# Transposing a masked attention matrix in 32x32 blocks on VectorE and moving the blocks by DMA, in a two-layer graph kernel

## The reference

```python
# layer 0: 4 heads of 64, mask adj[g]
h = relu(layernorm(x))
q, k, v = h @ Wq, h @ Wk, h @ Wv
att = softmax(where(adj, q @ k.T / 8, -FLT_MAX))
x = x + (att @ v) @ Wo + bo
# layer 1: 8 heads of 64, masked where adj is true
h = relu(layernorm(x))
m = h @ map_w.T + map_b
n = m / max(norm(m per head), eps)
cos_adj = (n @ n.T masked) > 0.1
q, k = m @ q_w.T + q_b, m @ k_w.T + k_b
p = softmax(where(mask, -1e10, q @ k.T / 8)) * keep
adj = cos_adj * p
out = relu(((adj @ (h @ gcn_map.T + b)) @ gcn_W.T) / (adj.sum(-1) + 1))
x = x + out
```

## Time and profile before

| | |
|---|---|
| median of 3 runs | 4121.55 us (4118.8 to 4130.23) |
| profiled execution | 4121.26 us, its span 4119.5 us |
| mean granted clock of TensorE | 0.993 |
| PE busy | 95%, 32976 matmuls |
| DVE busy | 63% |
| ACT busy | 48% |
| POOL busy | 32% |
| DMA queue of SP | 110.12 MB, 7.8% of 16 engines |
| x, out, move: each x64, 512 KB | 3.4, 2.8 and 3.1 us from issue to landing |
| adj: x64, 64 KB | 2.6 us from issue to landing |

### The profile page before, as it was taken

How to read it: one execution, slowest core, us unless ns; L and a number is a source line. 1 busy time by engine, 2 the same in 40 slices (tenths; PEclk the granted TensorE clock), 3 DMA queues, 4 the chain that set the end, 5 groups by cost and what they waited for, 6 DMA issues and landing times.

```text
span 4119.5 us, 105002 instructions
## 1 busy us (share of the span) xinstructions
PE 3931.4 (95%) x32976; PEld 3437.0 (83%) x32976; DVE 2608.3 (63%) x9426; ACT 1979.3 (48%) x5583; POOL 1324.3 (32%) x2007
## 2 busy tenths in 40 slices
PE   7999999999999999999999999999999999999997
PEld 6888888888888888888888888888888888888886
DVE  4666666666666666666666666666666666666664
ACT  3554544544545445445454454454454544544544
POOL 3333333333332333333333333333333333333332
PEclk8999999999999999999999999999999999999998
DMA  3000000000000000000000000000000000000000
GB/s 87 16 32 26 22 32 16 32 32 16 32 27 21 32 18 30 32 16 32 29 18 32 22 25 32 16 32 32 16 32 27 21 32 16 32 32 16 32 27 17
DMA packets 65544, 111.77 MB, mean 27 GB/s; under 512 B 20880, under 2 KB 22448, under 8 KB 65520
## 3 DMA queue, kind: packets, MB, share of 16 engines
q1 hardware_dynamic: 64928, 110.12, 7.8%
q0 software_dynamic: 592, 1.35, 0.2%
HBM read 44.34 MB, written 33.55 MB: 19 GB/s over the span
## 4 chain that ended last, share of the span: by engine, by line
PE 65%; DVE 12%; issue 11%; ACT 6%; POOL 4%; DVEq 1%; DMA 1%; POOLq 0%; ACTq 0%; SPq 0%
PE bank L755 34%; PE bank L763 9%; PE bank L748 7%; PE bank L783 6%; PE bank L775 4%; ACT prob L501 3%; PE bank L883 3%; POOL prob L417 2%; DVE x_mid L663 2%; ACT att L475 2%; DVE prob L650 2%; DVE att L607 2%; DVE att L618 1%; POOL rstd L362 1%; DVE hT L640 1%
## 5 line engine op out<-in xcount | busy, mean ns | idle before, releaser
L475 ACT ACTIVATE att<-att,nmax 128x256 f32<-128x256 f32 x1024 | 509.7, 500 | 299.6 <-DVE nmax L607 299.6
L417 POOL TENSOR_SCALAR prob<-prob,rsum 128x256 f32<-128x256 f32 x512 | 241.1, 487 | 631.2 <-DVE rsum L657 628.2
L755 PE MATMUL bank<-hT,w_qkv 128*128 128x256 f32 x3072 | 414.9, 288 | 4.7 <-DVE hT L640 4.7
L755 PE MATMUL bank<-qkm,w_k 128*128 128x256 f32 x3072 | 416.6, 285 | 0.0
L755 PEld LDWEIGHTS bank<-hT,w_qkv 128*128 128x128 f32 x3072 | 376.9, 189 | 37.9 <-issue 24.2
L755 PE MATMUL bank<-hT,w_map 128*128 128x256 f32 x3072 | 396.7, 285 | 5.1 <-DVE hT L640 1.0
L618 DVE SCALAR_TENSOR_TENSOR att<-bank,att 128x256 f32<-128x256 f32 x1024 | 392.3, 420 | 4.0
L755 PE MATMUL bank<-qkm,w_q 128*128 128x256 f32 x3072 | 390.8, 283 | 0.0
L755 PEld LDWEIGHTS bank<-hT,w_map 128*128 128x128 f32 x3072 | 372.5, 189 | 18.4 <-DVE hT L640 17.3
L763 PE MATMUL bank<-w_v,hT 128*128 128x512 f32 x1536 | 385.3, 399 | 0.0
L755 PEld LDWEIGHTS bank<-qkm,w_k 128*128 128x128 f32 x3072 | 380.1, 188 | 5.0
(11 more groups left out here) (122 smaller groups left out, 7949.6 us busy)
## 6 DMA issues: line engine op xcount, KB each, us to landing
x_in<-x SPq DMA_DIRECT2D x64, 512.0 KB, 3.4
x_res<-x_mid SPq DMA_DIRECT2D x64, 512.0 KB, 3.1
out<-x_res SPq DMA_DIRECT2D x64, 512.0 KB, 2.8
adj<-adj SPq DMA_DIRECT2D x64, 64.0 KB, 2.6
att<-gcn_map POOLq DMA_DIRECT2D x2, 512.0 KB, 9.0
x_mid<-wq SPq DMA_DIRECT2D x1, 512.0 KB, 5.6
x_res<-wk SPq DMA_DIRECT2D x1, 512.0 KB, 6.8
v<-wv SPq DMA_DIRECT2D x1, 512.0 KB, 7.7
```

The lines of the kernel that those rows point to most:

```text
L417: last = g.tensor_scalar(prob0[:, hd, c, :], prob0[:, hd, c, :], rsum0[:, hd, c:c + 1], 0.0, ALU.mult, ALU.add)
L475: s_.activation(e_sl, e_sl, ACT.Exp, bias=nmax1[:, p, c, e:e + 1], scale=-1.0, accum_out=esum1[:, p, c, e:e + 1]).then_inc(exp1_done, 1)
L755: last = t_.matmul(dst, w(ws, k)[:, t * 128:t * 128 + 128], rhs[:, rs, k, :], start=(k == 0 and i == 0), stop=(k == KT - 1 and i == 2))
```

## The change

The steps `turn_a` and `turn_b` are gone from TensorE and ScalarE. VectorE has the steps `flip_a` and `flip_b` in their place, one block transpose a head, in place in att: each 32x32 block of the 128x512 values is turned where it lies. Then each block column still has to move to the partition quarter where its row index is now: SP has a step `shift` a pair, 16 DMAs from `att` to `uT`, each from one quarter of 32 partitions to another (or the same), 1 KB a partition, 32 KB in all. A shift begins when both flips of its pair are done and the value product of the pair before has read uT. TensorE's `value` waits until all 16 have landed, and so does `score_a` of the pair after next, which writes the same half of att. So that a DMA finds its 256 numbers in one run, att is laid out with the four blocks quarters outermost, and the operands of score, cos and value are read in runs of 32 columns. `value` and `back` share bank 4, the plain steps have three banks (5 to 7), and all five lists are written anew.

```diff
@@ the lists: one line of TENSOR, and SYNC
-        "ht0a", ("score", 0), "ht0b", ("cos", 0), "qk0", "qk1", ("turn_a", 0), "qk2", ("turn_b", 0), "s0", "s1", ("value", 0),
+        ("score", 0), "ht0a", "ht0b", ("cos", 0), ("score", 1), "qk0", "qk1", "qk2", "qk3", "s0", "s1", ("cos", 1),
...
-    PBANKS = 4
+    PBANKS = 3
     SYNC = [
-        "x", ("out", 0), "move", "adj"
+        ("shift", 0), ("shift", 1), ("shift", 2), "x", ("shift", 3), ("out", 0), "adj", "move"
     ]
...
-        att = sb("att", [128, 2, 2, C, N])
+        att = sb("att", [128, 2, 4, 2, C, C, 32])
...
-        v_bank = gram_bank
+        v_bank = (bank[4], bank[4])
@@ SP
+                    elif kind == "shift":
+
+                        sp.wait_ge(flipped, pairs(a, p, 2) + 2)
+                        sp.sem_inc(passed_sync, 1)
+                        sp.wait_ge(uv_full, pairs(a, p))
+                        sp.sem_inc(passed_sync, 1)
+                        for rows in range(4):
+                            for cols in range(4):
+                                sp.dma_start(uT_blocks[32 * cols:32 * cols + 32, rows, :, :, :, :].rearrange("p e c j f -> p (e c j f)"),
+                                             att[32 * rows:32 * rows + 32, p % 2, cols, :, :, :, :].rearrange("p e c j f -> p (e c j f)")).then_inc(turned[p], 16)
@@ GpSimd
-                        g.tensor_scalar(mask1[:, :, :], adj8[:, :, :], MASKED_L1, 0.0, ALU.mult, ALU.add).then_inc(mask1_ready, 1)
+                        for c in range(C):
+                            g.tensor_scalar(mask1[:, c, :].rearrange("p (b j f) -> p b j f", j=C, f=32),
+                                            adj8[:, c, :].rearrange("p (j b f) -> p b j f", j=C, f=32), MASKED_L1, 0.0,
+                                            ALU.mult, ALU.add).then_inc(mask1_ready, 1)
@@ ScalarE
-                            e_sl = att[:, p % 2, e, c, :]
+                            e_sl = att[:, p % 2, :, e, c, :, :].rearrange("p b j f -> p b (j f)")
...
-                    elif kind in ("turn_a", "turn_b"):
-                        e = "ab".index(kind[5])
-                        act.wait_ge(t_full, pairs(a, p, 2) + e + 1)
-                        act.wait_ge(uv_full, pairs(a, p))
-                        s_.activation(uT[:, e, :], t_bank[e][:, :], ACT.Copy).then_inc(uT_ready, 1)
@@ VectorE
+                        if e == 0:
+                            dve.wait_ge(turned[(p + 2) % 4], BLOCK_MOVES * (a + (1 if p < 2 else 2)))
+                            dve.sem_inc(passed_vector, 1)
...
+                    elif kind in ("flip_a", "flip_b"):
+
+                        e = "ab".index(kind[5])
+                        dve.wait_ge(gated, pairs(a, p, 4) + 2 * e + 2)
+                        dve.sem_inc(passed_vector, 1)
+                        blocks = att[:, p % 2, :, e, :, :, :].rearrange("p b c j f -> p b (c j f)")
+                        v_.transpose(blocks, blocks).then_inc(flipped, 1)
@@ TensorE
+            def by_quarter(ap, source):
+
+                return ap.rearrange("p (j b f) -> p b j f", j=C, f=32) if source else ap.rearrange("p (b j f) -> p b j f", j=C, f=32)
...
-                            last[e] = t_.matmul(banks[e][:, c * N:c * N + N], left[r, ls, c * 128:c * 128 + 128], right[r, rs, :],
-                                                start=(i == 0), stop=(i == 2))
+                            last[e] = t_.matmul(order(banks[e][:, c * N:c * N + N], False), left[r, ls, c * 128:c * 128 + 128],
+                                                order(right[r, rs, :], True), start=(i == 0), stop=(i == 2))
...
-                        pe.wait_ge(uT_ready, pairs(a, p, 2))
-                        head_products(score_bank, q1[:, :, p, :], k1[:, :, p, :])[1].then_inc(score_full, 1)
+                        pe.wait_ge(masked, pairs(a, p, 4))
+                        head_products(score_bank, q1[:, :, p, :], k1[:, :, p, :], by_quarter)[1].then_inc(score_full, 1)
...
+                    elif kind == "value":
+                        pe.wait_ge(turned[p], BLOCK_MOVES * (a + 2))
                         pe.wait_ge(rel_done, pairs(a, p))
...
-                        values(v_bank[0][:, 0:N], v1, 2 * p, lambda e, jc: uT[:, e, jc * N:jc * N + N]).then_inc(uv_full, 1)
+                        values(v_bank[0][:, 0:N], v1, 2 * p, lambda e, jc: uT_blocks[:, :, e, :, jc, :].rearrange("p r c f -> p c r f")).then_inc(uv_full, 1)
```

More of the change, by code:

```diff
@@ L62, in gnn_two_layers @@
-        ("turn_b", 2), ("value", 2), "ht1a", "ht1b", ("exp_a", 3), "m0", ("exp_b", 3), "m1", ("turn_a", 3), "m2",
-        ("turn_b", 3), "m3", "q2", ("value", 3), "q1", "k1", "q0", "k0", "q3", "k3", "k2"
[4 rows of a table added]
     ]
     VECTOR = [
-        "ht0a", "ht0b", ("score_a", 0), ("score_b", 0), ("cos_a", 0), "qk0", ("cos_b", 0), "qk1", "s0", "qk2", "s1",
-        ("factor", 0), "sum0", ("back", 0), "sum1", "qk3", ("score_a", 1), ("score_b", 1), "s2", ("cos_a", 1), "s3",
-        ("cos_b", 1), "sum2", "sum3", "v0", ("factor", 1), ("back", 1), "av", ("score_a", 2), ("score_b", 2), ("cos_a", 2),
[3 rows of a table removed]
+        ("score_a", 0), ("score_b", 0), "ht0a", "ht0b", ("cos_a", 0), ("flip_a", 0), ("cos_b", 0), "qk0", ("flip_b", 0),
@@ L72, in gnn_two_layers @@
+        ("score_a", 1), "qk1", "qk2", ("score_b", 1), ("factor", 0), "qk3", "s0", ("cos_a", 1), "s1", "sum0", "s2", "s3",
+        ("flip_a", 1), "sum1", ("cos_b", 1), "sum2", ("flip_b", 1), "sum3", "v0", ("back", 0), ("factor", 1), ("score_a", 2),
+        ("score_b", 2), ("cos_a", 2), ("cos_b", 2), ("flip_a", 2), ("factor", 2), "av", ("flip_b", 2), ("score_a", 3),
[3 rows of a table added]
     ]
     POOL = [
-        ("unit", 0), "mid", "mask0", "sum0", "sum1", ("unit", 1), ("back", 0), "sum2", "sum3", "rstd1", ("back", 1),
@@ L75, in gnn_two_layers @@
-        ("back", 2), "m0", "rstd0", "m1", "m2", "m3", "pow", "mask1", ("back", 3)
+        "mask0", ("unit", 0), "mid", ("unit", 1), "sum0", "sum1", "sum2", "sum3", ("back", 0), "rstd1", ("back", 1), "m0",
+        "m1", ("back", 2), "mask1", "rstd0", "m2", "m3", "pow", ("back", 3)
     ]
-    PBANKS = 4
+    PBANKS = 3
     SYNC = [
-        "x", ("out", 0), "move", "adj"
+        ("shift", 0), ("shift", 1), ("shift", 2), "x", ("shift", 3), ("out", 0), "adj", "move"
     ]
     PRODUCTS = [s for s in TENSOR if isinstance(s, str)]
-    bank_of = {s: 4 + k % PBANKS for k, s in enumerate(PRODUCTS)}
+    bank_of = {s: 5 + k % PBANKS for k, s in enumerate(PRODUCTS)}
@@ L230, in gnn_two_layers @@
         gated = count("gated")
-        t_full = count("t_full")
-        uT_ready = count("uT_ready")
+        flipped = count("flipped")
+        turned = [count(f"turned{p}") for p in range(PAIRS1)]
         uv_full = count("uv_full")
@@ L286, in _ @@
                 sp.dma_start(adj8[:, :, :], adj[0].rearrange("(c p) j -> p c j", p=128)).then_inc(adj_loaded, 16)
+                for p in range(PAIRS1):
+                    sp.sem_inc(turned[p], BLOCK_MOVES)
                 for k, (src, _) in enumerate(PIECES):
@@ L856, in body @@
                         for t in range(PAIRS0):
-                            last = values(full[:, t * N:t * N + N], v0, 2 * t, lambda e, jc: ptm[:, 2 * t + e, jc * N:jc * N + N])
+                            last = values(full[:, t * N:t * N + N], v0, 2 * t, lambda e, jc: ptm[:, 2 * t + e, jc * N:jc * N + N].rearrange("p (c r f) -> p c r f", c=C, f=32))
                         last.then_inc(product_full, 1)
```

42 lines of the change are left out of this document (15 added, 27 removed), and 11 rows, old and new, of tables (SCALAR, TENSOR, VECTOR).

## The result

| | before | changed |
|---|---|---|
| median | 4121.92 us (4118.8 to 4130.23) | 5755.16 us (5753.48 to 5755.82) |
| ratio, 95% interval | | 1.3957 (1.3933 to 1.3981) |
| span of the profiled execution | 4119.5 us | 5753.0 us |
| mean granted clock | 0.993 | 0.843 |

The changed kernel is 39.6% slower: 1633 us, some 25.9 us for each of the 63 loop bodies where the forecast had 15.7. The direction was right, the size was not, and the time lies above the range's end of 5470.

The account below looks back on a forecast made before the run. TensorE's queue was taken as the bound: 57.6 us work, 16.0 waits and 5.3 clock make 78.9 a graph, 15.7 more; 4121 + 989 (63 bodies) + 15 = 5125 us. Range 4330 to 5470.

Parts of the forecast that it names:

- What bounds the kernel, what goes: TensorE's queue sets the end; 32 att transposes (3.5 us) and 2.1 us of waits go, leaving 57.6 us a graph.
- the two waits of 2.1 us: TensorE waits 0.74 us before pair 2's value product and 1.36 before the transposes of h; both subtracted.
- rival 1: Small DMAs issue much quicker, a shift lasts 4.6 us or less; 58.7 us a graph, 3845 us in all; chance 0.17.
- VectorE: Eight block transposes a graph at 0.65 us, 5.2 us (3.4 to 11.2), within its idle time; strided reads cost nothing.
- Rival 3: Reads in runs of 32 slow TensorE, or VectorE's transposes are at their upper price; 5470 us; chance 0.05.
- SP: Sixteen DMAs a pair issued one by one, 0.48 us each plus landing 1.9: a shift of 9.1 us (7.3 to 10.7).
- What hides a shift: TensorE stalls 3.0, 3.7, 4.1 and 4.5 us at value products, plus 0.7 for hT: 16.0, so 73.6 a graph.
- The walk: Stepping the new queues from score 0 to place each shift's landing against TensorE's arrival at the value product.
- The clock: The granted clock falls at each stall; slower TensorE work costs 5.3 us a graph (0 to 8), making 78.9.
- The sum: 63 loop bodies at 15.7 us more each, 989, plus 15 for the last graph's second layer: 5125 us.
- Rival 2: Slower, but less: issue takes 0.37 to 0.42 or the clock holds; 4330 or 4790 us; chance 0.30.
- Its point of decision: Rival 1 decides at TensorE's value products: four stalls eating at most 4.9 us, a shift of 6.5, an issue of 0.31.

Follow-up runs that it names:

- the run with filler work: Changed kernel plus 40 to 52 unread identity transposes on TensorE ahead of each value product's wait: 5394.93 us, ratio 1.3083, clock 0.995.
- the way through HBM: Changed kernel with blocks moved by one 512 KB store to HBM and four 128 KB loads, 5 DMAs a pair instead of 16: 4529.79 us, 1.099.
- the best of those run: Changed kernel with two uT buffers and value products later in the lists, all 64 block moves a graph kept: 4199.29 us, ratio 1.0177.

## Why the prediction was wrong in size

- **What bounds the kernel, what goes.** Right. TensorE's own work without the transposes was put at 57.6 us and is 57.8. But the two waits of 2.1 us were taken as gone. With one move a pair 3.5 us of waits are there, four of the five at places where TensorE didn't wait before; 58.7 a graph was 61.4, and rival 1's 3845 was 4003. This did not touch the forecast, where the stalls hide them: it made the good case look better than it was.
- **VectorE.** 0.65 taken as the step; the next one starts 0.63 behind a flip. VectorE is at 52%. The strided reads cost nothing, as taken. Rival 3 is out. The flips themselves are cheap, save for what they may hold up in VectorE's queue; what is dear is to finish them. The Trainium skill (VectorE: DVE Perf Modes, Rules for kernel authors) sends a 128x128 transpose to TensorE where PSUM will do as its destination, and leaves VectorE the 32x32 ones. The runs agree: the 3.5 us a graph of TensorE came back as four moves of 11.3.
- **SP: this step failed.** "I take 0.48, the row of the same kind." The issues come 0.631 apart, and even the upper bound of 0.54 was too low. The row of x_res from x_mid is of a DMA that stands alone in the queue; in the changed kernel, where it follows adj at once, even this one takes 548 ns. That a step of 0.045 lies between two issues was left out as well, though the chain would show it and the loads at the start, 0.45 long, began 0.49 apart in the same rows. There was a sign that an issue isn't always as short as where it stands alone: adj, 0.39 in the loop, took 0.45 in that row. The landing, 1.9, was exact. A shift so lasts 11.3 and not 9.1 us.
- **What hides a shift.** The walk was right: four stalls a graph, and 4 us a graph for each us of shift. The longer shift put into it gives 15 x 0.151 x 4 = 9.1 us more a graph. The table below has it place by place: where the clock was kept up, each of the four distances is within 0.3 us of the walk's. That is nearly all of the error: 73.6 + 9.1 = 82.7, and 88.8 less that leaves 6.1 for the clock. Before value 2 the uT buffer held shift 2 for 3.1 us, as the walk had it.
- **The clock.** It falls at each of the four stalls. 5.3 forecast, 5.7 by the run with filler work, 6.1 by the difference above. The last two columns of the table put 2.5 of it behind value 3 and 1.6 behind value 2, where the forecast had 2.3 and 1.0.
- **The sum.** 63 x (9.1 + 6.1 - 5.3) = 624 of the 630 us that were missed; the longer shifts of the last graph are the rest.
- **Rivals.** Rival 1 needed an issue of 0.31 or less; a block move took 0.59 from SP and 0.50 from GpSimd, and only the large store and loads of the way through HBM, at 0.34 and 0.43, were nearer. Its point of decision, a shift of 6.5 us, was put too high: with eight moves (a shift of 6.3 us) the kernel should have been just faster than before and is 2.6% slower. A graph takes 64.2 us there, 58.7 of work and 5.5 of waits, where the walk gives 57.6, 4.1 and 0.7; it had left out the clock and a part of the waits for VectorE. Rival 2 had both the clock and the issue too cheap.
- **The range.** It was built from the durations of single rows. The bound that was missing is that of a row of issues, which the trace of before had only with loads from HBM. And its upper end was rival 3's time, not the sum of its own upper bounds: a shift of 10.7 and a clock of 8 would have given 5125 + 63 x (4 x 1.6 + 2.7) = about 5700, 230 us above the 5470 and 1% below the measured time.

The distances in us from one value product to the next, by the walk's landings and by the rows of the two timelines:

| from value to value | walk, issues 0.48 apart | walk, 0.631 apart | measured, clock kept up | measured, changed kernel |
|---|---|---|---|---|
| 2 to 3 | 13.35 | 15.6 | 15.86 | 17.45 |
| 3 to 0 | 37.5 | 39.8 | 39.62 | 42.12 |
| 0 to 1 | 12.55 | 14.8 | 14.93 | 15.81 |
| 1 to 2 | 10.2 | 12.5 | 12.54 | 13.40 |
| sum | 73.6 | 82.7 | 82.95 | 88.78 |

## What to carry to other kernels

Before a transfer is cut into many small ones, count issues, not bytes: n issues in one queue last n times the distance between two of them, and that distance is read from a row of issues of the same kind of memory, not from one that stands alone. If such a row is in a chain, spread it over queues that have nothing urgent behind it, make fewer and larger DMAs even by a longer way, or move the consumer later. And taking work off the bounding engine can take away cover too: list the latencies that it hid before counting all of it as gain; here, with a new order and with the flips on VectorE, 5.6 us of removable time were worth 1.8.

## What was not expected of the hardware

- The issue of a block move inside SBUF takes 0.59 us (0.631 apart), with 128 B a partition as with 1 KB. In the way through HBM it is 0.34 for the store and 0.43 for the loads, and 0.50 where GpSimd issues the same block moves. Where the two sides are isn't all of it: x_res from x_mid, inside SBUF too, takes 0.48 alone and 0.548 behind adj. These DMAs differ in shape and partitions as well, which no run separates.
- Issues of two engines run beside each other without slowing each other: SP's block moves take 590 ns with GpSimd's beside them, and 591 without.
- The granted clock was 0.50 behind the waits of 4.8 to 6.5 us in the changed kernel's loop body, and the steps behind one of 4.03 (value 1 moved behind ht1b) took as long.
- The first two DMAs in the row shown are issued faster (0.54 and 0.58) than those after them (0.59).

What stays open: why the block moves' issue inside SBUF is longer than the issues to and from HBM, what the 3.5 us of waits with one move come from, and whether lists exist in which both the shifts and the latencies around the layer norm are covered; the best of those run (4199 us) is 1.8% slower than the kernel before, and none beats it with all of the work done.
